# A decoder kernel: softmax maxima turned into rows by VectorE through DRAM in one cross attention, written into PSUM by ScalarE in the other

## The reference, cut to what matters

```
s = q @ k.T                      # scores
p = exp(s - max(s)) ; out = (p @ v) / p.sum()
```

## Time and profile before

| | us |
|---|---|
| median of 3 runs | 736.56 |
| lowest and highest | 735.44, 743.9 |
| the profiled execution, device time | 738.48 |
| its span, first to last instruction | 736.7 |
| busy in it: PE, DVE, ACT, POOL | 627.8, 530.2, 427.7, 206.8 |
| mean granted TensorE clock, share of full speed | 0.939 |

### The profile page before, as it was taken

How to read it: one execution, slowest core, us unless ns; L and a number is a source line. 1 busy time by engine, 2 the same in 40 slices (tenths; PEclk the granted TensorE clock), 3 DMA queues, 4 the chain that set the end, 5 groups by cost and what they waited for, 6 DMA issues and landing times. The chain is left out here.

```text
span 736.7 us, 13537 instructions
## 1 busy us (share of the span) xinstructions
PE 627.8 (85%) x5184; PEld 343.4 (47%) x5184; DVE 530.2 (72%) x705; ACT 427.7 (58%) x769; POOL 206.8 (28%) x251
## 2 busy tenths in 40 slices
PE   7978899999999999999997568997447789969996
PEld 5644433333333333333333246884123467637884
DVE  5368789999999999999842358996596467746342
ACT  3545478888888888888873224555842022244224
POOL 7217432343343665554300020000000560005000
PEclk9998989999999999999999579999769699989999
DMA  8357575555555435435100357540000400000000
GB/s 198 116 123 225 150 231 179 141 132 123 151 153 153 122 100 105 91 95 99 44 2 0 87 213 319 156 145 0 0 0 1 157 1 1 1 0 0 1 1 28
DMA packets 41084, 70.76 MB, mean 96 GB/s; under 512 B 11332, under 2 KB 30108, under 8 KB 40512
## 3 DMA queue, kind: packets, MB, share of 16 engines
q1 hardware_dynamic: 30128, 33.98, 18.3%
q0 software_dynamic: 10288, 33.71, 14.3%
q10 hardware_dynamic: 608, 2.25, 1.4%
HBM read 44.84 MB, written 24.79 MB: 95 GB/s over the span
## 5 line engine op out<-in xcount | busy, mean ns | idle before, releaser
L908 ACT ACTIVATE prob<-ps 128x512 f32<-128x512 f32 (+2 forms) x480 | 253.3, 582 | 48.9 <-PE ps L703 41.0
L1027 DVE TENSOR_REDUCE pm<-ps 128x2 f32<-128x1024 f32 x192 | 226.2, 1216 | 9.0 <-PE ps L665 7.2
L726 PE MATMUL ps<-prob,vst 128*9 128x256 f32 (+1 forms) x1664 | 130.1, 385 | 10.1 <-ACT o_all L896 10.1
L703 PE MATMUL ps<-qq,kc 50*128 50x256 bf16 (+1 forms) x832 | 133.7, 275 | 0.1
L665 PE MATMUL ps<-kc,qq 48*128 48x512 bf16 x384 | 116.9, 391 | 5.4 <-DVE pm L1027 4.3
L703 PEld LDWEIGHTS ps<-qq,kc 50*128 50x128 bf16 (+1 forms) x832 | 52.0, 96 | 93.7 <-ACT prob L908 69.9
L726 PEld LDWEIGHTS ps<-prob,vst 128*9 128x9 f32 (+1 forms) x1664 | 25.1, 88 | 51.7 <-ACT prob L908 39.1
L1839 ACT ACTIVATE prob<-s 128x512 f32<-128x512 f32 (+1 forms) x28 | 15.9, 567 | 56.7 <-PE s L1771 53.9
L1034 DVE TENSOR_REDUCE nm<-ps 128x4 f32<-128x512 f32 (+1 forms) x32 | 30.7, 958 | 15.3 <-PE ps L653 15.3
L665 PEld LDWEIGHTS ps<-kc,qq 48*128 48x128 bf16 x384 | 33.0, 94 | 16.5 <-DVE pm L1027 10.7
L1705 POOL MEMSET pick<- 128x128 f32 x1 | 0.2, 205 | 134.4 <-SPq L1702 134.4
(11 more groups left out here) (354 smaller groups left out, 1318.4 us busy)
## 6 DMA issues: line engine op xcount, KB each, us to landing
kc<-kc_scr SPq DMA_DIRECT2D x32, 300.2 KB, 4.9
comb_bc<-comb_scr SPq DMA_DIRECT2D x8, 512.0 KB, 4.6
kc_scr<-hi POOLq DMA_DIRECT2D x9, 400.2 KB, 4.1
below<-rden_scr POOLq DMA_DIRECT2D x13, 256.0 KB, 9.0
ctx<-ctx_scr POOLq DMA_DIRECT2D x1, 3204.0 KB, 16.3
raw<-in_wexp POOLq DMA_DIRECT2D x8, 384.0 KB, 3.5
exp_scr<-raw_high POOLq DMA_DIRECT2D x8, 384.0 KB, 5.0
exp_scr<-raw_low POOLq DMA_DIRECT2D x8, 384.0 KB, 6.8
```

Of the source, the lines that this page charges most:

```text
L703: last = pe.matmul(bank[0:p, j * TQ:(j + 1) * TQ], kc[s][rows, j, t * 128:t * 128 + p], qq[s][rows, 0, j, :], start=(j == 0), stop=True, s ...
L726: last = pe.matmul(o_ps[32 * hh:32 * hh + VW, kind * TQ + q0:(kind + 1) * TQ], value[:, hh * VW:(hh + 1) * VW], prob[0:k, (NST * n + t) % ...
L908: act.activation(prob[0:p, g % P_RING, 2 * e:2 * e + 2, q0:TQ], s2[0:p, k % S2_RING, 0:2 * w].rearrange("p (i q) -> p i q", i=2), ACT.Exp, ...
L1027: dve.tensor_reduce(pm[:, m % 2, c, :, jt], banks, AX.X, ALU.max).then_inc(s1_read, 1)
```

## The change

In the first cross attention `turn_maxima`, its place in `s1_order` and the bank reads go. `nm` becomes the first 16 columns of a zeroed tile [128, 32]. `row(m)`, now called directly after `combine(m)` and so ahead of half 0 of the next unit, transposes the four 32x32 blocks of this tile on DVE, copies the result as bf16 and subtracts it for the rest, all in SBUF. The blocks hold 32 queries each, so the rows have to be put together: SP writes `mrow` to a DRAM tensor `mrow_scr` (one DMA of 128 runs of 128 bytes), issues the two key loads of unit m+2, waits until the first DMA has landed (`rows_out`), and brings the rows into `qq` by four DMAs of 32 pieces of 64 bytes each. The six `load_split` DMAs follow. For the last two units there are no loads between.

In the second cross attention `pick` and its three memsets on POOL go. `max_row` broadcasts to 128 columns, so the row arrives in all partitions of `fin`; `row(b)` is one fp32 copy of [128, 256], called ahead of the last `add` of the batch. ACT copies it into the `s2` bank (`shifts(k)`) two steps ahead, right after the exponential that empties the bank, and PE's `scores_t` waits for that (`filled`) and accumulates onto it.

```diff
-            s1_order = []
-            for m in range(NU):
-                s1_order.append((m, 0))
-                if m:
-                    s1_order.append((m - 1, TURN))
...
             def wait_s1_free(engine, n):
                 if n < 2:
                     engine.wait_ge(x_ready, n + 1)
-                m, i = s1_order[n - 2]
-                if i == TURN:
-                    engine.wait_ge(mrow_ready, m + 1)
                 else:
-                    engine.wait_ge(s1_read, HALVES * m + i + 1)
+                    engine.wait_ge(s1_read, n - 1)
...
-                    def max_rows(m):
+                    def max_rows_out(m):
+                        sp.wait_ge(mrow_ready, m + 1)
+                        sp.dma_start(mrow_scr[m], mrow[m % SLOTS][:]).then_inc(rows_out, 16)
+
+                    def max_rows_in(m):
                         s = m % SLOTS
-                        sp.wait_ge(mrow_ready, m + 1)
+                        sp.wait_ge(rows_out, 16 * (m + 1))
+                        rows = mrow_scr[m].rearrange("(k e i) p r -> p e i k r", k=4, e=4)
                         for e in range(2):
                             for part in range(2):
                                 at = GROUP * e + ROWS + part
-                                sp.dma_start(qq[s][at:at + 1, :, :, :].rearrange("o k j (t q) -> o (k j t) q", t=2),
-                                             mrow[s][8 * e:8 * e + 8, part, :]).then_inc(max_in[s], 16)
+                                sp.dma_start(qq[s][at:at + 1, :, :, :].rearrange("o k j (t n r) -> o (k j t) n r", t=2, n=4),
+                                             rows[part, e].unsqueeze(0)).then_inc(max_in[s], 16)
...
                         load_context(n)
+                        if m is not None:
+                            max_rows_in(m)
                         for kind in X_KINDS:
                             load_split(kind, n)
...
                     for m in range(NU):
-                        max_rows(m)
+                        max_rows_out(m)
                         if m + 2 < NU:
-                            load_unit(m + 2)
+                            load_unit(m + 2, m)
+                        else:
+                            max_rows_in(m)
...
-                    def turn_maxima(m):
-                        n = s1_at[m, TURN]
-                        wait_s1_free(pe, n)
-                        pe.wait_ge(nm_ready, m + 1)
-                        pe.transpose(s1[0:16, n % 2, 0, 0:128], nm[:].rearrange("p e k i -> p (e k i)"), ident).then_inc(s1_ready, 1)
...
                     def row(m):
-                        n, u = s1_at[m, TURN], m % SLOTS
-                        dve.wait_ge(s1_ready, n + 1)
-                        dve.tensor_copy(mrow[u][:, 0, :], s1[0:16, n % 2, 0, 0:128]).then_inc(m1_done, 1)
+                        u = m % SLOTS
+                        dve.wait_ge(nm_ready, m + 1)
+                        dve.transpose(nm_turned[:], nm_all[:]).then_inc(nm_turns, 1)
+                        dve.wait_ge(nm_turns, m + 1)
+                        dve.tensor_copy(mrow[u][:, 0, :], nm_turned[:]).then_inc(m1_done, 1)
                         dve.wait_ge(m1_done, m + 1)
-                        dve.tensor_tensor(mrow[u][:, 1, :], s1[0:16, n % 2, 0, 0:128], mrow[u][:, 0, :],
-                                          ALU.subtract).then_inc(mrow_ready, 1)
+                        dve.tensor_tensor(mrow[u][:, 1, :], nm_turned[:], mrow[u][:, 0, :], ALU.subtract).then_inc(mrow_ready, 1)
...
                             reduce_half(m, i)
-                            if m and i == 0:
-                                row(m - 1)
...
                         combine(m)
-                    row(NU - 1)
+                        row(m)
```

The second cross attention:

```diff
-                pool.memset(pick[:].bitcast(F32), 0.0).then_inc(set_up, 1)
...
-                        o = fin[0:33, t * 128:(t + 1) * 128]
-                        pe.matmul(o, nm_b[:, n:n + 1].to_broadcast([128, 33]), ident, start=True, stop=False)
+                        o = fin[:, t * 128:(t + 1) * 128]
+                        pe.matmul(o, nm_b[:, n:n + 1].to_broadcast([128, 128]), ident, start=True, stop=False)
...
                 def scores_t(b, p):
                     k = b * PAIRS + p
-                    if k >= 2:
-                        pe.wait_ge(exp_done, k - 1)
+                    pe.wait_ge(filled, k + 1)
-                    if 2 * p + 1 < NKT:
-                        pe.matmul(s2[:, k % 2, :].rearrange("p (i q) -> p i q", i=2), pick[:],
-                                  shift[:, at].unsqueeze(1).to_broadcast([128, 2, TQ]), start=True, stop=False,
-                                  skip_group_check=True)
...
+                def shifts(k):
+                    b, p = divmod(k, PAIRS)
+                    m, sides = (128, 2) if 2 * p + 1 < NKT else (KLAST, 1)
+                    act.wait_ge(row_sb, b + 1)
+                    if k < 2:
+                        act.wait_ge(qk_sb, k + 1)
+                    else:
+                        act.wait_ge(exp_done, k - 1)
+                    act.activation(s2[0:m, k % 2, 0:sides * TQ].rearrange("p (i q) -> p i q", i=sides),
+                                   shift[0:m, b % 2, :].unsqueeze(1).to_broadcast([m, sides, TQ]), ACT.Copy).then_inc(filled, 1)
...
                                        ACT.Exp).then_inc(exp_done, 1)
+                        if p < PAIRS - 2:
+                            shifts(k + 2)
+                    if b + 1 < NB:
+                        for p in range(2):
+                            shifts((b + 1) * PAIRS + p)
...
                 def row(b):
-                    at = slice(b * TQ, (b + 1) * TQ)
                     dve.wait_ge(row_ps, b + 1)
-                    if b == 0:
-                        dve.wait_ge(set_up, 3)
-                    dve.tensor_copy(shift[0:33, at], fin[0:33, 0:TQ]).then_inc(row_high, 1)
-                    dve.wait_ge(row_high, b + 1)
-                    dve.tensor_tensor(shift[32:33, at], fin[32:33, 0:TQ], shift[32:33, at], ALU.subtract).then_inc(row_sb, 1)
+                    dve.tensor_copy(shift[:, b % 2, :], fin[:, 0:TQ]).then_inc(row_sb, 1)
...
                     for p in range(PAIRS):
+                        if b + 1 < NB and p == PAIRS - 1:
+                            row(b + 1)
                         add(b, p)
...
-                    if b + 1 < NB:
-                        row(b + 1)
```

More of the change, by code:

```diff
@@ L51 @@
 SLOTS = 4
-HALVES, TURN = 15, -1
+HALVES = 15
 P_RING, S2_RING = 4, 3
@@ L202, in decoder_program @@
             pm = held(st, "pm", [128, 2, 4, 2, 4])
-            nm = held(st, "nm", [128, 2, 2, 4])
-            mrow = [held(st, f"mrow{s}", [16, 2, 128], BF16) for s in range(SLOTS)]
+            nm_all, nm_turned = (held(st, n, [128, 32]) for n in ("nm", "nm_turned"))
+            nm = nm_all[:, 0:16].rearrange("p (e k i) -> p e k i", e=2, k=2)
+            mrow = [held(st, f"mrow{s}", [128, 2, 32], BF16) for s in range(SLOTS)]
             ps = st.enter_context(nc.psum_tensor("ps1", [128, 8, 512], F32))
@@ L737, in half @@
                         score_part(m, i, 0).then_inc(s1_ready, 1)
-                        if i == 0 and m:
-                            turn_maxima(m - 1)
                     def scores_and_half(g, h):
@@ L756, in scores_and_half @@
                         scores_t(n, t, 1, 1)
-                        if more and i == 0:
-                            turn_maxima(m - 1)
-                        if h == NU * HALVES:
-                            turn_maxima(NU - 1)
                     pe.wait_ge(masks_cast, 1)
@@ L1678, in emit_rest @@
         qk_high, qk_low = (sb(f"qk_{part}", [2 * CC, T], F32R) for part in ("high", "low"))
-        shift = sb("shift6", [128, T], F32R)
-        pick = sb("pick6", [128, 128], F32R)
+        shift = sb("shift6", [128, 2, TQ])
         bkq = sb("bkq6", [128, 2 * NB])
@@ L1704, in _ @@
             def _(pool):
-                pool.memset(pick[:].bitcast(F32), 0.0).then_inc(set_up, 1)
-                pool.wait_ge(set_up, 1)
-                pool.memset(pick[0:1, :].bitcast(F32), 1.0)
-                pool.memset(pick[32:33, :].bitcast(F32), 1.0).then_inc(set_up, 1)
-                pool.wait_ge(set_up, 2)
-                pool.memset(shift[:].bitcast(F32), 0.0).then_inc(set_up, 1)
                 for n in FFN_WEIGHTS:
@@ L1748, in max_row @@
                         n = 2 * b + t
-                        o = fin[0:33, t * 128:(t + 1) * 128]
-                        pe.matmul(o, nm_b[:, n:n + 1].to_broadcast([128, 33]), ident, start=True, stop=False)
-                        last = pe.matmul(o, col["bk6"].to_broadcast([128, 33]), q[:, n * 128:(n + 1) * 128],
+                        o = fin[:, t * 128:(t + 1) * 128]
+                        pe.matmul(o, nm_b[:, n:n + 1].to_broadcast([128, 128]), ident, start=True, stop=False)
```

(11 more changed lines are left out.)

30 lines of the change are left out of this document (15 added, 15 removed).

## The result

The changed kernel took 770.07 us in the median of 4 runs, the kernel before 736.75 in 4 beside it; the ratio is 1.0416, with a 95% interval from 1.0317 to 1.0515. It is slower by over 4%, where I had forecast 733. Three of its runs lie between 766.7 and 772.7; the fourth, 1138.72 us, was a disturbed execution and is left out of the ratio.

What follows compares the result with a forecast made beforehand. The first cross attention was taken as bound by engines waiting for each other, the second by PE. Terms -7.0 + 4.5 + 6.0 - 7.0 = -3.5 us gave 735.0 against the profiled execution, 733 for the median; range 721 to 748.

Steps and rivals of the forecast that it cites:

- loop, quiet: First cross attention's unit boundary: one PE step less, half 0 reduced later; gain 0.47 us per boundary, 7.0 us in all.
- GpSimd holds DVE's row: First cross attention: DVE's subtraction, perhaps its copy, waits while GpSimd works; costs 4.5 us, bounds 0 and 9.
- the way of the rows: Maxima through DRAM into qq: late in busy units, 1 us in 6 of 14 units; costs 6 us, bounds 0 to 28.
- second cross attention: Pick matmul gone and ACT filling the bank: three batches give 4.8 us, the start 2.2; gain 7.0 us, bounds 2 to 10.
- quiet budget: Rows' way through DRAM in a quiet unit: 6.4 us from first issue to landing, against 6.95 us available.
- landing of 2.2 us: Time taken for a row DMA to land, from the nearest write to DRAM; used for the way out and the gather.
- Rival 2: Rows late in every unit, at 8.5 us costing 22 us over 14 units; 749 us in all; chance 0.16.
- deciding point of 7.6 us: Rows' way above which the kernel gets slower than before, from 9.5 us net gain spread over 14 units.
- DVE's lag: First cross attention: DVE takes 1.13 us against PE's 1.10, lagging 0.03 a step, given back by masked and copy steps.
- Rival 4: First cross attention: the two-bank order makes half 2 wait just as long, loop gain 0; 740 us; chance 0.07.
- The pick's 0.34 us a step: Second cross attention: the pick matmul's cost per step, whose removal saves 1.9 us a batch.
- Rival 3: Second cross attention: ACT's fills don't hide, 1.4 us a step, the block gains only 2 us; 738 us; chance 0.08.

Runs made afterwards that it cites:

- run 7: Run 4 with DVE's copy and subtraction of the turned maxima replaced by three short reductions over one or two elements; 733.53 us, ratio 0.9935.
- run 4: The changed kernel, but from the third unit on each unit takes the maxima of two units earlier, so rows are never late; 738.06 us, ratio 0.9999.
- run 1: The kernel before with only the second cross attention's part of the change; 734.46 us, ratio 0.9968.
- run 3: The changed kernel with the four row DMAs issued ahead of the two key loads instead of behind them; 758.67 us.
- run 8: The changed kernel with one bf16 row of maxima, no copy or subtraction, two row DMAs instead of four, ahead of the keys; 720.84 us, ratio 0.9797.
- run 11: Run 3 with copy and subtraction replaced by three short reductions, all maxima those of their own unit; 758.09 us, ratio 1.0291.
- run 12: Run 11 with GpSimd's split expert weight loads and stores narrowed to 64 columns from expert 2 on, plus one bulk copy; 758.75 us, ratio 1.0277.

## Why the prediction was wrong

By the runs the parts are these, in us. A check on them: 737.33 - 4.4 - 2.4 + 3.8 for run 7's longer chain is 734.3, and run 7 took 733.53. The 8.3 and the 2.4 are each known to some 3 us only.

| step of the prediction | forecast | measured | from |
|---|---|---|---|
| loop, quiet | -7.0 | -4.4 | 18.375 against 18.67, 15 times |
| GpSimd holds DVE's row | +4.5 (0 to 9) | +8.3 | runs 4 and 7 |
| the way of the rows | +6.0 (0 to 28) | +32.0 | the changed kernel and run 4 |
| second cross attention | -7.0 (2 to 10) | -2.4 (-3.8 by the traces) | run 1 |

**The way of the rows is the step that failed.** I laid out a quiet budget, 6.4 us against 6.95, and took 1 us in 6 of 14 units. By the trace's packets the last piece ended 5.5 to 10.5 us after the way out was issued in the 14 units with keys ahead, and 6.6 and 5.0 in the two without. The landing of 2.2 us that I took for the gather came from a plain write; and I let the keys' 4.9 us run beside the rows, while their 600 KB went through the same queue first (run 3 took them out of the way, for 11 us by the medians).

Rival 2 is what happened, and its way of pricing was right. In the 14 units with keys ahead the unit's first scores came 7.0 to 11.4 us after the way out was issued, 9.2 in the mean, and 7.07 in the undisturbed units of run 4. (9.2 - 6.95) x 14 is 31 us, against the 32.0 measured; its 22 came from 8.5 us taken for these 9.2. Its deciding point of 7.6 us was wrong, since it rested on 9.5 us of net gain elsewhere: run 4, with rows that are never late, shows none, so here any lateness is a loss.

No term of the sum had the granted clock. Between 75 and 410 us it stood at 0.50 for 51 us in the changed kernel, 20 in run 4 and 17 before. In the stretch of the earlier trace rows it was 0.91 with 21.7 us of waits for rows, 0.95 in run 3 with 10.8, and 1.00 in run 7 with one wait of 2.7 and in run 8 with none. It does not go by late rows alone: run 4 has 0.98 with 1.2 us of them, and one of its falls comes behind a held copy, after which three PE steps take 1.94 us in place of 1.13. What it costs can be bounded from the trace of the changed kernel. Each wait for the rows ended with their landing, so slow steps before it cost nothing more. Outside the way of the rows, from a unit's first scores to the next issue out, 14 boundaries lengthen by 12.9 us over the 11.31 of an undisturbed one, and 7.1 of these are the held operations. So the slower steps have at most some 6 us. No run separates them further.

**GpSimd's hold.** The mechanism was right and undersized. The copy from SBUF is held too, which I had left half open: up to 1.55 us beside a GpSimd operation, where the reductions of run 7 kept to 186 ns beside the same work. The Trainium skill (SBUF — State Buffer, Who interferes with whom) has both halves of this, copies and casts able to take the shared ports and reductions never contending; by that rule the term was 7.4, and the traces agree with 7.1 in the operations themselves, 6.6 in run 4. The rest of the 8.3 us lies within its spread, or behind them, as in the unit of run 4 whose copy was held by 1.3 us: it took 22.6 us, 4.2 over an undisturbed one, with the clock at 0.50 for 6.8 us of it.

**The loop.** PE's step at half 1 went from 2.206 to 1.09 us, the predicted 1.1. Half 2's step went from 1.09 to 1.81, so the later half 0 costs 0.72 there, where I had 0.63. The three steps behind it take 1.13 us instead of 1.09, at DVE's pace: another 0.11, which I had seen as DVE's lag and set to nothing. The transposition was 0.21, as I took it, copy and subtraction 0.18 and 0.19, each 0.02 more. In a quiet unit half 0 is reduced 0.81 us after the combination began, kernel after in order of time:

```profile
142.23 0.21 DVE L1029 TENSOR_REDUCE nm<-pm 128x8 f32<-128x32 f32 x1
...
142.94 0.19 DVE L1039 TENSOR_TENSOR mrow<-nm_turned,mrow 128x32 bf16<-128x32 f32 x1
143.04 4.62 DVE L1016 TENSOR_REDUCE pm<-ps 128x2 f32<-128x1024 f32 x4
...
144.32 0.39 PE L663 MATMUL ps<-kc,qq 48*128 48x512 bf16 x1 [0.44 <-DVE pm L1016]
...
145.45 0.39 PE L663 MATMUL ps<-kc,qq 48*128 48x512 bf16 x1
```

That is 0.69 later than before instead of 0.63. In all 1.12 - 0.72 - 0.11 is 0.29, the gain measured. Rival 4 is out, the wait did shorten.

**The second cross attention.** The pick's 0.34 us a step gave 0.24: steady steps take 1.245 us, not 1.14, since the first matmul of a group is now followed by the second only after 0.23 us (673.00 to 673.23; 0.20 in the row below), where it was 0.12 behind the pick. Kernel after, order of time:

```profile
640.51 0.36 PE L1744 MATMUL s<-qk_high,ctx 128*128 128x256 f32 x1 [0.67 <-ACT s L1811]
640.71 0.28 PE L1744 MATMUL s<-qk_low,ctx 128*128 128x256 f32 x1
640.82 0.28 PE L1744 MATMUL s<-qk_high,ctx 128*128 128x256 f32 x1
```

The same row shows the second loss: at the head of a batch PE waits 0.67 us for ACT's fill. A middle batch takes 14.75 us for 15.5 before, 0.75 less and not the 1.6 of the forecast. The start gave nothing, since in it DVE's `nm_b` waits for GpSimd as before; up to the second batch's first exponential 1.1 us are gained for 2.2 forecast:

```profile
620.09 1.89 POOL L1696 CAST high_h1w<-w_h1w 128x2048 fp32r<-128x2048 f32 x1
620.48 1.51 DVE L1872 TENSOR_TENSOR nm_b<-nm,bkq 128x1 f32<-128x1 f32 x1
```

From first scores to last exponential the block is 3.9 us shorter in the changed kernel's profile and 3.8 in that of run 1, whose median gives 2.4. Rival 3 (2 us) came nearer in size than the forecast, but not by what it named: no step takes its 1.4 us.

**The range.** I gave rival 2 0.16, and called 2.2 us the row that spoke against it. The end of 28 us that I had written for the rows never entered the range: the forecast with it is 733 + 22 = 755, still 15 short.

## What to carry to other kernels

Before a step goes through DRAM, count what stands ahead of it in its own queue and what another queue may send meanwhile, and compare that, not the quiet sum, with the slack; 0.5 us of slack on a way of 6.4 us is none. Put the small transfer that an engine waits for ahead of the large one that nobody waits for yet, and make it contiguous: alone they gave 11.4 and 2.8 us (the second within the spread, and with a longer way out), together 24.5, and 19 by the ratios. A small DVE operation on a critical path beside busy GpSimd is best a reduction or a transposition; and what is best of all is to need neither copy nor split, as in run 8.

## What was unexpected in the hardware

- DVE's 128x32 transposition was never held by GpSimd, in any of 16 in each trace: 210 to 215 ns, f32 and bf16 alike. In every trace with it, 5 to 10 of them ran beside a GpSimd operation that went on past their end, as the one at 165.25 did.
- A `tensor_reduce` over one element is a copy with conversion for 186 ns, against 180 for the free copy and 1553 for the held one.
- A DMA that is first in its own queue, 128 pieces of 64 B, ended 5.0 us after the way out was issued with no keys and nothing from GpSimd beside it (unit 15 of the changed kernel) and 10.2 beside 1.0 MB of another queue's transfers (unit 4 of run 11, where another unit with as much ended at 6.2). The Trainium skill (DMA: Bandwidth & Descriptors, Queues, rings and completion order) says that each DMA engine goes round between the queues it has work for, a packet of several descriptors at a time; that would let another queue's large pieces stand between small ones, and units 2 to 6 of run 12 agree with it. No run here shows the order of pieces within an engine.
- A standstill of PE of under 2 us (until 168.44) was followed by about 3 us at half clock.
